# A fused two-layer block on one core: batch 1's value tiles projected one head later and in other PSUM banks

## The chip, the cores and the metric

The kernel runs on one core of one Trainium2 chip. The metric is device microseconds for one execution of the whole kernel. A trace of one execution was taken by the hardware profiler; the engines are TensorE (PE, with its weight loads PEld), VectorE (DVE), ScalarE (ACT), GpSimd (POOL) and SyncE (SP, which issues the DMA transfers).

## The reference, cut to what matters

The block runs cross-attention, a quantised feed-forward, a second attention layer that has a self-attention ("a1") and a cross-attention ("a2"), each with its own feed-forward, and a last feed-forward. The change lies wholly within the self-attention a1: 2 batches, 512 tokens of 128 features, 16 heads of 32 features, so 32 pairs of batch and head.

```python
xn = _ln(x, lnx_g, lnx_b)
yn = _ln(y, lny_g, lny_b)
q = jnp.einsum('bsc,hcd->bhsd', xn, wq)
k = jnp.einsum('btc,hcd->bhtd', yn, wk)
v = jnp.einsum('btc,hcd->bhtd', yn, wv)
a = jax.nn.softmax(jnp.einsum('bhsd,bhtd->bhst', q, k) * D ** (-0.5), axis=-1)
if causal:
    a = a * mask
o = jnp.einsum('bhst,bhtd->bhsd', a, v)
```

For a1, x and y are the same tensor and `causal` is true; the mask keeps only keys after the query (`t > s`).

## The kernel before, in words

The order of the work is written out by hand, one program per engine; an engine runs its instructions in that order and waits on semaphores. There are eight PSUM banks of 128 x 512 values: S0 to S3 for the scores, T0 and T1 for transposes, A and B for the rest. A bank is claimed by TensorE (`claim`), which waits until the bank's last reader has released it.

In a1 the loop runs over n = 0 to 33; head n (below, "head 8" is n = 8) is a pair of batch and head, 16 heads of batch 0 first. Per head:

- TensorE multiplies four tiles of queries with all keys (`scores`, L702, banks S0 to S3, one per tile). The float32r operands lie in `stack`, where each head's high and low halves of q and k are stacked.
- VectorE takes each row's negated maximum (L1647); ScalarE computes the exponential with its row sum (L1247); GpSimd masks the diagonal block (L1009).
- One head later TensorE transposes the ten kept 128 x 128 blocks of the weights (`p_transposes`, L444 with `pring`) in three sets of 4, 3 and 3 blocks. The sets alternate between T0 and T1 (`next_T`). ScalarE copies the first set into the ring PT (L1231), VectorE the second (L1619), and the third goes to ScalarE after an odd head, to VectorE after an even one.
- Every four heads form a group k. At n % 4 == 1 TensorE transposes the inverse row sums (`sums_transposes`, L444 with `xn`, bank A), ScalarE copies them (`sums_across`, L1211); at n % 4 == 2 and 3 the weighted values follow in bank A (`values`, L738), and VectorE multiplies the two (`normalise`, L1639).

Beside this loop the operands of later heads are made. At even n from 6 to 20 one 128 x 512 projection of q or k is computed in bank B (`project`, L688); in the next head ScalarE writes its high half (L1203), VectorE its low half (`low_half`, L1592), and when a set of four projections is complete, SyncE stacks the halves with four transfers per pair of heads (L884, 256 KB each). Head 8, 16 and 24 are the first ones to read the next stacked set, and each waits for it by a semaphore (`stacked[0]`).

The values V of 8 tiles of 128 tokens are projected by `project_values` (one float32 projection, 128 x 512, in two passes, L761). Tiles 0 to 3 (batch 0) come ahead of the loop and in head 0. Tiles 4 to 7 (batch 1) are given by `value_tile(n)`: in the kernel before at n = 8, 12, 16 and 20, in bank A, which is free then between the weighted values of one group and the sums of the next. They are copied in the head that follows, n = 9, 13, 17 and 21: even tiles by ScalarE (L1216) behind its copy of the first set of transposes, odd ones by VectorE (L1599) behind its copy of the second set. The first reader of tiles 4 to 7 is the weighted values of head 22.

```python
def next_T():
    turn[0] += 1
    return f"T{turn[0] % 2}"

def project_values(t, res):
    pe.wait_ge(ynT_ready, t // NT + 1)
    claim(pe, res, ("v", t), read_by=((V_act, V_dve)[t % 2], t // 2 + 1))
    filled(pe.matmul(bank(res), ynT[:, t // NT, t % NT * P:(t % NT + 1) * P], wa1_sb[:, 2, :],
                     start=True, stop=True), ("v", t))
```

Of the kernel before, what the change touches and what calls it, by code (L numbers as in the profile page):

```python
# [39 lines left out]
NT = 4  # L40
# [42 lines left out]
def build(nc, x, ctx_in, w64, w128, wf0, wa1, wa2, wa2kv, wf1, rows, cols, out):  # L83
    with ExitStack() as st:
# [104 lines left out]
        def bank(res):  # L189
            return ps[:, BANKS[res], :]  # L190
# [60 lines left out]
        def claim(pe, res, key, read_by=None, filled_by=None):  # L251

            if res in last:
                pe.wait_ge(*last[res])
            if read_by is None:
                frees[res] += 1
                read_by = (bank_free[res], frees[res])
            if filled_by is None:
                fulls[res] += 1
                filled_by = (bank_full[res], fulls[res])  # L260
            where[key], filled_when[key], read_when[key], last[res] = res, filled_by, read_by, read_by

        def filled(ins, key):

            return ins.then_inc(filled_when[key][0], 1)
# [149 lines left out]

        def value_tile(n):

            return NT + n // 4 - 2 if n % 4 == 0 and 8 <= n <= 20 else None

        def pt_base(n):  # L420

# [18 lines left out]
        def _(pe):  # L440
# [249 lines left out]
            def scores(n, i):  # L690

                b, j, e, _ = head(n)
                claim(pe, f"S{i}", ("s1", n, i), read_by=(exp1_done, NT * n + i + 1))
                if i == 0:
                    if n < 2:

                        pe.wait_ge(first_stack[n], 16 * 4)
                    elif e == 0:

                        t = n // (2 * HG)  # L700
                        pe.wait_ge(stacked[j], stack_count(t, j))
                filled(pe.matmul(bank(f"S{i}"), stack[:, j, 0, e, i * P:(i + 1) * P], stack[:, j, 1, e, :],  # L702
                                 start=True, stop=True), ("s1", n, i))
# [47 lines left out]
            def sums_transposes(k):  # L751
                pe.wait_ge(rdx_ready, k + 1)
                res = "A" if k < NGRP - 1 else "B"
                claim(pe, res, ("rt", k), read_by=(RT_ready, k + 1))
                transposes(("rt", k), res, lambda t: rdx[:, t, :, :].rearrange("p h d -> p (h d)"), NT)
# [7 lines that stand above are left out]
# [19 lines left out]
            for n in range(NHB + 2):  # L782
                k = n // HG - 1
                if n < NHB:
                    scores(n, 0)
                    scores(n, 1)
                if 1 <= n <= NHB:
                    p_transposes(n - 1, 0)
                    p_transposes(n - 1, 1)
                if n >= HG and n < NHB and n % HG == 3:  # L790
                    values(k, (2,))
                if n == 0:
                    project_values(2, "T0")
                if n < NHB:
                    scores(n, 2)
                    scores(n, 3)
                if n == 0:
                    project_values(3, "T1")
                if 1 <= n <= NHB:
                    p_transposes(n - 1, 2)  # L800
                if n >= HG and n % HG == 1:
                    sums_transposes(k)
                if n >= HG and n % HG == 2:
                    values(k, (3,))
                if n >= HG and n < NHB and n % HG == 3:
                    values(k, (1, 0))
                if n == NHB + 1:
                    values(k, (3, 2, 1, 0))
                for m, res in next_projections(n):
                    project(m, res)  # L810
                if n == 4:
                    ln_transposes("a1", 1)
                if value_tile(n):
                    project_values(value_tile(n), "A")
                if n == NHB:
                    li1(0)

# [217 lines left out]
        def _(act):  # L1035
# [177 lines left out]
            def copy_values(t):  # L1213
                key = ("v", t)
                res = await_bank(act, key)
                release(act.activation(V[:, t, :], bank(res), ACT.Copy), key)  # L1216
# [21 lines left out]
            for n in range(NHB + 2):  # L1238
                if 1 <= n <= NHB:
                    pt_copy(n - 1, 0)  # L1240
                if value_tile(n - 1) and value_tile(n - 1) % 2 == 0:
                    copy_values(value_tile(n - 1))
                for u in range(2):
                    if n < NHB:
                        for i in range(2 * u, 2 * u + 2):
                            act.wait_ge(nm1_ready, NT * n + i + 1)
                            release(act.activation(pring[:, n % 2, i, :], bank(f"S{i}"), ACT.Exp,  # L1247
                                                   bias=nm1[:, n % 8, i:i + 1], accum_out=den1[:, n % 8, i:i + 1]),
                                    ("s1", n, i))
                    if u == 0 and 1 <= n <= NHB and n % 2 == 0:  # L1250
                        pt_copy(n - 1, 2)
                    if u == 0:
                        for m, _ in next_projections(n - 1):
                            high_half(m)
                    if u == 0 and n in (5, 6):
                        a1_evac(1, "qk"[n - 5])
                if n == 0:
                    copy_values(2)
                if n >= HG and n % HG == 1:
                    sums_across(n // HG - 1)  # L1260

# [25 lines left out]
        def _(dve):  # L1287
# [297 lines left out]
            def low_half(m):  # L1585

                which, e, t = projection(m)
                scale = float(D1) ** -0.5 if which == "q" else 1.0
                dve.wait_ge(hi_ready, m + 1)
                halves_free(dve, m)  # L1590
                res = await_bank(dve, ("qk", m))
                ins = dve.scalar_tensor_tensor(part(which + "l", t)[:, e, :], bank(res), scale,  # L1592
                                               part(which + "h", t)[:, e, :].bitcast(F32), ALU.mult, ALU.subtract)
                release(ins, ("qk", m))

            def copy_values(t):
                key = ("v", t)
                res = await_bank(dve, key)
                release(dve.tensor_copy(V[:, t, :], bank(res)), key)  # L1599
# [42 lines left out]
            for n in range(NHB + 2):  # L1642
                for u in range(2):
                    if n < NHB:
                        for i in range(2 * u, 2 * u + 2):
                            await_bank(dve, ("s1", n, i))
                            dve.tensor_reduce(nm1[:, n % 8, i:i + 1], bank(f"S{i}"), AX.X, ALU.max,  # L1647
                                              negate=True).then_inc(nm1_ready, 1)
                    if 1 <= n <= NHB and (u == 0 or n % 2):
                        pt_copy(n - 1, 1 + u)  # L1650
                    if u == 0 and HG <= n <= NHB and n % HG == 0:
                        inverse_sums(n // HG - 1)
                    if u == 0 and value_tile(n - 1) and value_tile(n - 1) % 2:
                        copy_values(value_tile(n - 1))
                for m, _ in next_projections(n - 1):
                    low_half(m)
                if n == 0:
                    copy_values(3)
                    ln_stats("a1", 1, x1)
                if n == 2:  # L1660
                    ln_norm("a1", 1, x1)
                if n >= HG and n < NHB and n % HG == 3:
                    normalise(n // HG - 1)
                if n == NHB:

                    for j in range(HG):
                        dve.wait_ge(stacked[j], stack_count(3, j))
                    for b in range(NB):
                        did(dve.tensor_tensor(xb[:, b, :, :], x1[:, b, :, :], row4("a1_li1_b"), ALU.add))
                    settle()  # L1670

                    add_to_xb(0, "li1")
                    ln_stats("a1f", 0, xo)
                if n == NHB + 1:
                    normalise(NGRP - 1)
# [127 lines left out]
```

## Time and profile before

| what | us |
|---|---|
| median of 3 runs | 386.19 (384.49 to 387.12) |
| profiled execution, whole time | 386.85 |
| its span, first to last instruction | 385.1 |
| TensorE busy in the span | 330.1 (86%) |
| VectorE busy | 285.7 (74%) |
| ScalarE busy | 271.5 (70%) |
| GpSimd busy | 122.7 (32%) |

The trace's times are counted from the span's start. Busy times are shares of the whole span, an average over stages with different limits. Matmuls are pipelined: the duration of one includes the time until its result has left the array, so several in a row overlap, and the start of the next tells more than the end of the last. A row's idle time is that of its engine ahead of it, with the instruction that ended it. In the trace head 8 starts at 152.58 us, head 12 at 169.48, head 16 at 185.87, head 20 at 202.77 and head 24 at 219.26; the value copies are those at 158.29 and 191.6 (ScalarE) and at 175.60 and 208.90 (VectorE).

### The profile page before, as it was taken

To read this page: it belongs to the slowest core of one execution; us is meant where nothing else is said; L and a number is where in the kernel's file an instruction comes from. 1 tells how busy PE (TensorE), PEld (TensorE's weight loads), DVE (VectorE), ACT (ScalarE), POOL (GpSimd) and SP (SyncE) were. 2 spreads that over 40 slices of the span, in tenths; PEclk is the share of its full clock that TensorE was granted. 3 is DMA by queue.
4 is the path that set the end of the run, shared out by engine and by line. 5 is a ranking of instruction groups with operands and counts; after the bars stand their busy time and mean duration, and the time that the engine had idled before them with its cause. 6 is when DMAs were issued, how large, how long until landed. Compare 5 with 4: busy or idle time off the path is not lost.

```text
span 385.1 us, 6932 instructions
## 1 busy us (share of the span) xinstructions
PE 330.1 (86%) x2165; PEld 233.5 (61%) x2165; DVE 285.7 (74%) x736; ACT 271.5 (70%) x957; POOL 122.7 (32%) x227
## 2 busy tenths in 40 slices
PE   5989999717698888898999889899896999978993
PEld 4868887503334554555646555576674888765673
DVE  0767779597886995979979889855586887846515
ACT  2378897847364998989999899914248888754441
POOL 1317665236512332223233233311023533421200
PEclk9999999968898999999999999999998999999999
DMA  6900000000019869403970896000000000000001
GB/s 197 361 9 1 2 3 0 0 1 3 0 43 211 184 143 211 84 2 69 212 159 1 178 212 214 3 2 0 2 2 1 1 2 0 3 0 2 0 2 54
DMA packets 6908, 24.75 MB, mean 64 GB/s; under 512 B 1451, under 2 KB 1528, under 8 KB 6136
## 3 DMA queue, kind: packets, MB, share of 16 engines
q1 hardware_dynamic: 6872, 24.31, 26.3%
q8 instruction: 18, 0.29, 0.3%
q14 instruction: 18, 0.15, 0.1%
HBM read 7.00 MB, written 0.52 MB: 20 GB/s over the span
## 4 chain that ended last, share of the span: by engine, by line
PE 45%; DVE 23%; ACT 16%; DMA 5%; issue 5%; SPq 3%; POOL 1%; DVEq 0%; ACTq 0%
PE ps L444 7%; PE ps L568 7%; PE ps L546 7%; ACT pring L1247 6%; PE ps L626 5%; PE ps L608 5%; DVE nm L1647 4%; PE ps L475 3%; SPq L884 3%; ACT arena L1121 3%; PE ps L496 3%; DMA stack<-sides 3%; PE ps L702 2%; ACT arena L1231 2%; PE ps L738 2%
## 5 line engine op out<-in xcount | busy, mean ns | idle before, releaser
L1647 DVE TENSOR_REDUCE nm<-ps 128x1 f32<-128x512 f32 x128 | 81.2, 678 | 17.0 <-PE ps L702 17.0
L1247 ACT ACTIVATE pring<-ps,nm 128x512 f32<-128x512 f32 x128 | 89.0, 725 | 6.4 <-DVE nm L1647 6.4
L1121 ACT ACTIVATE arena<-ps,nmx 128x77 f32<-128x77 f32 x256 | 79.2, 344 | 14.4 <-DVE nmx L1417 14.1
L1009 POOL TENSOR_SCALAR_AFFINE_SELECT pring<-pring 128x128 f32<-128x128 f32 x128 | 37.4, 295 | 80.9 <-ACT pring L1247 80.9
L702 PE MATMUL ps<-stack 128*128 128x512 f32 x128 | 55.2, 491 | 5.8 <-ACT pring L1247 2.4
L1121 ACT ACTIVATION_READ_ACCUMULATOR arena<-ps,nmx 128x1 f32 x256 | 57.2, 223 | 0.0
L974 POOL TENSOR_TENSOR arena<-arena,rden 128x616 f32<-128x616 f32 x32 | 39.2, 1226 | 51.3 <-DVE rden L1426 51.3
L444 PE MATMUL ps<-ident,pring 128*128 128x128 f32 x320 | 46.9, 275 | 5.9 <-ACT arena L1231 4.3
L444 PEld LDWEIGHTS ps<-ident,pring 128*128 128x128 f32 x320 | 36.5, 140 | 19.8 <-POOL pring L1009 10.7
L568 PEld LDWEIGHTS ps<-arena 128*128 128x128 f32 x320 | 38.9, 191 | 13.1 <-DVE arena L1433 11.7
L568 PE MATMUL ps<-arena 128*128 128x128 f32 x320 | 42.5, 280 | 4.9 <-DVE arena L1433 4.9
L965 POOL TENSOR_TENSOR rstd<-var,minus_half 128x4 f32<-128x4 f32 x18 | 18.8, 1045 | 86.5 <-DVE var L1319 86.5
L546 PE MATMUL ps<-arena,xnT 128*128 128x308 f32 x128 | 39.7, 434 | 2.8 <-ACT arena L1121 1.8
L702 PEld LDWEIGHTS ps<-stack 128*128 128x128 f32 x128 | 22.2, 190 | 27.6 <-ACT pring L1247 16.5
L1433 DVE COPY arena<-ps 128x384 f32<-128x384 f32 x64 | 28.0, 478 | 11.9 <-PE ps L444 11.9
L1231 ACT ACTIVATE arena<-ps 128x512 f32<-128x512 f32 (+1 forms) x48 | 28.6, 595 | 8.7 <-PE ps L444 8.7
L1417 DVE TENSOR_REDUCE nmx<-ps 128x8 f32<-128x616 f32 x32 | 25.5, 797 | 8.6 <-PE ps L546 8.2
L1247 ACT ACTIVATION_READ_ACCUMULATOR pring<-ps,nm 128x1 f32 x128 | 31.1, 243 | 0.0
L1147 ACT ACTIVATE hid<-ps,cols_sb 128x512 f32<-128x512 f32 x24 | 16.3, 686 | 20.1 <-PE ps L608 20.1
L444 PE MATMUL ps<-ident,arena 128*128 128x128 f32 x200 | 28.2, 277 | 1.6 <-POOL arena L974 0.6
L546 PEld LDWEIGHTS ps<-arena,xnT 128*128 128x128 f32 x128 | 22.2, 193 | 9.6 <-ACT arena L1121 2.8
L1619 DVE COPY arena<-ps 128x384 f32<-128x384 f32 x48 | 26.2, 546 | 0.1
(149 smaller groups left out, 525.9 us busy)
## 6 DMA issues: line engine op xcount, KB each, us to landing
stack<-sides SPq DMA_DIRECT2D x32, 256.0 KB, 5.0
stack<-arena SPq DMA_DIRECT2D x16, 256.0 KB, 5.1
stack<-hid SPq DMA_DIRECT2D x12, 256.0 KB, 5.0
wa_sb<-in_wa SPq DMA_DIRECT2D x1, 1536.0 KB, 14.1
early<-in_w SPq DMA_DIRECT2D x2, 512.0 KB, 8.0
stack<-hid SPq DMA_DIRECT2D x8, 128.0 KB, 2.5
arena<-in_wa SPq DMA_DIRECT2D x1, 1024.0 KB, 4.8
pring<-in_wf SPq DMA_DIRECT2D x1, 768.0 KB, 10.7
```

The source lines that it names most:

```text
L444: m = pe.transpose(bank(res)[0:width, t * parts:(t + 1) * parts], src(t), ident[0:parts, 0:parts])
L546: m = pe.matmul(bank(res)[:, 0:4 * HS].rearrange("p (h s) -> p h s", s=HS)[:, :, 0:M], xnT[:, b, t * P:(t + 1) * P], FK[:, b, c0:c0 + 4 * ...
L568: m = pe.matmul(bank(res)[:, t * P:(t + 1) * P], PTc[:, j % 4, k, :], VO[:, b, half * (NCH // 2) + k, :], start=(half == 0 and k == 0), st ...
L702: filled(pe.matmul(bank(f"S{i}"), stack[:, j, 0, e, i * P:(i + 1) * P], stack[:, j, 1, e, :], start=True, stop=True), ("s1", n, i))
L974: pool.tensor_tensor(pv, pv, rden[:, j % 4, :].unsqueeze(2).to_broadcast([P, 8, M]), ALU.mult).then_inc(pn_ready, 1)
L1009: pool.affine_select(out=blk, in_=blk, compare_op=ALU.is_gt, fill=0.0, base=0, pattern=[[1, P]], channel_multiplier=-1).then_inc(masked, 1)
L1121: ins = act.activation(Pc[:, i % PC_SLOTS, h * HS:h * HS + M], bank(where[key])[:, h % 4 * HS:h % 4 * HS + M], ACT.Exp, bias=nmx[:, i % 4, ...
L1231: release(act.activation(pt_piece(n, piece), src, ACT.Copy), key)
L1247: release(act.activation(pring[:, n % 2, i, :], bank(f"S{i}"), ACT.Exp, bias=nm1[:, n % 8, i:i + 1], accum_out=den1[:, n % 8, i:i + 1]), ( ...
L1433: release(dve.tensor_copy(PTc[:, j % 4, k0:k1, :].rearrange("p k n -> p (k n)"), bank(res)[:, 0:(k1 - k0) * P]), key)
L1619: release(dve.tensor_copy(pt_piece(n, piece), src), key)
L1647: dve.tensor_reduce(nm1[:, n % 8, i:i + 1], bank(f"S{i}"), AX.X, ALU.max, negate=True).then_inc(nm1_ready, 1)
```

## The change

`value_tile` now names n = 9, 13, 17 and 21. The projection takes the next bank of the weights' transposes instead of bank A. The copies move to the same n: on ScalarE behind the head's last exponential and ahead of the copy of the sums, on VectorE behind the low halves of the projection.

```diff
         def value_tile(n):
 
-            return NT + n // 4 - 2 if n % 4 == 0 and 8 <= n <= 20 else None
+            return NT + n // 4 - 2 if n % 4 == 1 and 9 <= n <= 21 else None
...
                 if value_tile(n):
-                    project_values(value_tile(n), "A")
+                    project_values(value_tile(n), next_T())
...
                 if 1 <= n <= NHB:
                     pt_copy(n - 1, 0)
-                if value_tile(n - 1) and value_tile(n - 1) % 2 == 0:
-                    copy_values(value_tile(n - 1))
                 for u in range(2):
...
                 if n == 0:
                     copy_values(2)
+                if value_tile(n) and value_tile(n) % 2 == 0:
+                    copy_values(value_tile(n))
                 if n >= HG and n % HG == 1:
                     sums_across(n // HG - 1)
...
                         inverse_sums(n // HG - 1)
-                    if u == 0 and value_tile(n - 1) and value_tile(n - 1) % 2:
-                        copy_values(value_tile(n - 1))
                 for m, _ in next_projections(n - 1):
                     low_half(m)
+                if value_tile(n) and value_tile(n) % 2:
+                    copy_values(value_tile(n))
```

On TensorE, the rows from the end of head 8 to the transposes of the sums in head 9 stood as follows. L688 is the projection of q or k, L761 that of the value tile 4, L702 the scores, L444 with `pring` the transposes of the weights and with `xn` those of the sums; in brackets are the semaphores that a row waits for (`V_act` and `V_dve` are counted up by the value copies, `pt_act` and `pt_dve` by the copies of the transposed weights, `exp1_done` by the exponentials).

```order
L688 MATMUL ps<-ynT,wa1_sb 128x512 [waits lo_ready,ynT_ready]
L761 MATMUL ps<-wa1_sb,ynT 128x512 [waits OT_ready,ynT_ready]
L702 MATMUL ps<-stack 128x512 [waits exp1_done] x2
L444 MATMUL ps<-ident,pring 128x128 [waits pt_dve,masked]
L444 MATMUL ps<-ident,pring 128x128 x3
L444 MATMUL ps<-ident,pring 128x128 [waits pt_act,masked]
L444 MATMUL ps<-ident,pring 128x128 x2
L702 MATMUL ps<-stack 128x512 [waits exp1_done] x2
L444 MATMUL ps<-ident,pring 128x128 [waits pt_act,masked]
L444 MATMUL ps<-ident,pring 128x128 x2
L444 MATMUL ps<-ident,xn 128x128 [waits V_act,rdx_ready]
L444 MATMUL ps<-ident,xn 128x128 x3
```

Here are the changed kernel's rows of the same engine from the third set of head 8's transposes to the second set of head 9's.

```order
L444 MATMUL ps<-ident,pring 128x128 [waits pt_act,masked]
L444 MATMUL ps<-ident,pring 128x128 x2
L444 MATMUL ps<-ident,xn 128x128 [waits OT_ready,rdx_ready]
L444 MATMUL ps<-ident,xn 128x128 x3
L761 MATMUL ps<-wa1_sb,ynT 128x512 [waits pt_dve,ynT_ready]
L702 MATMUL ps<-stack 128x512 [waits stacked1,exp1_done]
L702 MATMUL ps<-stack 128x512 [waits exp1_done]
L444 MATMUL ps<-ident,pring 128x128 [waits pt_dve,masked]
L444 MATMUL ps<-ident,pring 128x128 x3
L444 MATMUL ps<-ident,pring 128x128 [waits V_act,masked]
L444 MATMUL ps<-ident,pring 128x128 x2
```

The projection has moved from ahead of head 9's scores to behind the sums' transposes; the wait for the value copy has moved from those to the second set of head 9's transposes.

On VectorE, this is the difference in heads 13 and 14 (tile 5): L1647 are the maxima, L1619 the copies of the weights' transposes, L1592 the low half, L1599 the value copy.

```order
 L1647 TENSOR_REDUCE nm<-ps 128x1 x4
 L1619 COPY arena<-ps 128x3x128
+L1647 TENSOR_REDUCE nm<-ps 128x1 x2
+L1619 COPY arena<-ps 128x3x128
+L1592 SCALAR_TENSOR_TENSOR arena<-ps,arena 128x512
 L1599 COPY early<-ps 128x512
 L1647 TENSOR_REDUCE nm<-ps 128x1 x2
 L1619 COPY arena<-ps 128x3x128
-L1592 SCALAR_TENSOR_TENSOR arena<-ps,arena 128x512
-L1647 TENSOR_REDUCE nm<-ps 128x1 x2
-L1619 COPY arena<-ps 128x3x128
```

The value copy now stands behind two maxima, a copy and the low half, and ahead of the maxima of head 14. Heads 21 and 22 read the same, with `sides` in place of `arena` in the low half's row.

## Rows read from the trace of the kernel before

**Rows 1.** Busy time by stretch: us, then each engine's, clock, DMA share, GB/s

```profile
86.00:88.00 2.00, 1.44 (x7) 0.86 (x8) 0.51 (x2) 1.19 (x2) 1.40 (x1) 0.50 0.00 0
...
152.50:169.50 17.00, 16.02 (x115) 9.62 (x107) 14.71 (x27) 15.85 (x45) 5.23 (x17) 1.00 0.31 67
...
202.80:219.30 16.50, 14.41 (x109) 9.16 (x105) 15.94 (x29) 15.48 (x43) 5.72 (x19) 1.00 0.37 77
```

**Rows 2.** Chain of waits, two pieces: start us, us, what

```profile
162.54 0.50 ACT arena L1231
...
213.98 5.15 DMA stack<-sides
```

**Rows 3.** Timeline of TensorE, heads 8 to 13: start, us, instruction, idle before, releaser

```profile
154.88 1.02 PE L688 MATMUL ps<-ynT,wa_sb 128*128 128x512 f32 x2
155.74 1.02 PE L761 MATMUL ps<-wa_sb,ynT 128*128 128x512 f32 x2
...
159.04 0.63 PE L444 MATMUL ps<-ident,xn 128*128 128x128 f32 x4
...
160.28 0.50 PE L702 MATMUL ps<-stack 128*128 128x512 f32 x1 [0.17 <-ACT pring L1247]
160.62 0.93 PE L444 MATMUL ps<-ident,pring 128*128 128x128 f32 x7
...
162.11 0.51 PE L702 MATMUL ps<-stack 128*128 128x512 f32 x1 [0.17 <-ACT pring L1247]
163.18 0.52 PE L444 MATMUL ps<-ident,pring 128*128 128x128 f32 x3 [0.56 <-ACT arena L1231]
...
176.43 0.63 PE L444 MATMUL ps<-ident,xn 128*128 128x128 f32 x4 [0.47 <-DVE early L1599]
...
177.36 1.25 PE L444 MATMUL ps<-ident,pring 128*128 128x128 f32 x7
...
179.59 0.52 PE L444 MATMUL ps<-ident,pring 128*128 128x128 f32 x3 [0.52 <-ACT arena L1231]
```

**Rows 4.** Timeline of ScalarE, heads 9 and 13

```profile
158.29 0.61 ACT L1216 ACTIVATE early<-ps 128x512 f32<-128x512 f32 x1
...
161.89 0.65 ACT L1211 ACTIVATE xn<-ps 128x512 f32<-128x512 f32 x1
162.37 0.66 ACT L1231 ACTIVATE arena<-ps 128x512 f32<-128x512 f32 x1
...
176.51 0.62 ACT L1203 ACTIVATE arena<-ps 128x512 fp32r<-128x512 f32 x1
...
178.79 0.65 ACT L1231 ACTIVATE arena<-ps 128x512 f32<-128x512 f32 x1
```

**Rows 5.** Timeline of TensorE, first scores of head 24

```profile
219.26 0.70 PE L702 MATMUL ps<-stack 128*128 128x512 f32 x2 [0.88 <-DMA stack<-sides]
```

**Rows 6.** Timeline of VectorE, heads 10 and 13

```profile
165.81 1.29 DVE L1647 TENSOR_REDUCE nm<-ps 128x1 f32<-128x512 f32 x2 [1.51 <-PE ps L702]
...
175.60 0.68 DVE L1599 COPY early<-ps 128x512 f32<-128x512 f32 x1
176.20 1.28 DVE L1647 TENSOR_REDUCE nm<-ps 128x1 f32<-128x512 f32 x2
...
177.86 0.68 DVE L1592 SCALAR_TENSOR_TENSOR arena<-ps,arena 128x512 fp32r<-128x512 f32 x1
```

**Rows 7.** Timeline of VectorE, the low half in head 21

```profile
211.15 0.68 DVE L1592 SCALAR_TENSOR_TENSOR sides<-ps,sides 128x512 fp32r<-128x512 f32 x1
```

**Rows 8.** Timeline of SyncE's issues, 205 to 222 us

```profile
211.91 11.11 SPq L884 DMA_DIRECT2D stack<-sides  x10
```

**Rows 9.** Timeline of TensorE in the quantised feed-forward

```profile
85.27 0.61 PE L527 MATMUL ps<-identb,pring 128*128 128x128 bf16 x4 [4.96 <-ACT pring L1103]
86.56 1.03 PE L519 MATMUL ps<-wf0b,pring 128*128 128x512 bf16 x2 [0.69 <-ACT pring L1108]
...
91.13 0.59 PE L519 MATMUL ps<-wf0b,pring 128*128 128x512 bf16 x2
```

## Prediction

> **What bounds the kernel now.** I read the page's first part, then the busy time by stretch, the chain of waits, and last the timelines of the engines. On the page TensorE is the busiest engine, with VectorE and ScalarE not far behind; but shares of the whole span say little here, because all of the change lies between head 8 and head 24 of the first self-attention. So I cut that stretch at the first scores of every fourth head and read the busy time [rows 1]: of the 17.00 us of heads 8 to 11 TensorE works 16.02, ScalarE 15.85 and VectorE 14.71; heads 20 to 23 have TensorE at 14.41 of 16.50. All three are close to the bound, so moving work between queues without removing any can only win what somebody waits for. TensorE's granted clock is 1.00 in both, its upper level of 2.4 GHz.
>
> Who waits for whom is in the chain of waits [rows 2]. In the group of heads 8 to 11 it runs through ScalarE until its copy of head 9's first weights (L1231, 162.37), and goes over to TensorE at 163.18, which waited for that copy [rows 2, 3]. None of ScalarE's rows from 158.29 to that copy names idle time ahead of it [rows 4]. Before head 24 the chain lies on a transfer: the stacked halves of batch 1's second pair of groups land at 219.13, and TensorE, idle for 0.88 us, starts head 24 at 219.26 [rows 2, 5].
>
> **What the change touches there, and the sum.** Nothing is added or removed: four projections, four copies. The pairs of heads are 8 to 10 and 16 to 18 (tiles 4, 6, copied by ScalarE), 12 to 14 and 20 to 22 (tiles 5, 7, copied by VectorE); I work out one of each, the other repeats it in the trace to 0.1 us.
>
> The projection. A key projection of the same shape starts at 154.88 and the value projection behind it at 155.74, so one takes 0.86 us of TensorE's stream [rows 3]. It leaves the end of head 8. That is worth nothing there: ScalarE is full and VectorE's rows run on, so earlier scores of head 9 only lie in their banks longer. It comes back behind the transposes of the sums (159.04). There TensorE waits three times before 163.18: 0.17, 0.17 and 0.56, together 0.90 [rows 3]. So 0.86 fits.
>
> ScalarE, tile 4. Its copy holds a slot of 0.48 us at 158.29. It moves behind the last exponential of head 9, and what stood between slides 0.48 earlier; so it runs from 161.89 - 0.48 = 161.41 to 162.02 (it lasts 0.61). The sums' copy still starts at 161.89 and the copy of head 9's first weights at 162.37, because the work ahead of both is the same [rows 4]. The cost on ScalarE is 0.
>
> The new wait. The tile now occupies a bank of the weights' transposes, and the next but one in that ring, head 9's second set, must wait for the copy. Behind it in TensorE's queue stand head 10's last two scores, head 9's third set and the weighted values. A copy by ScalarE that started at 162.37 and lasted 0.66 let TensorE go at 163.18, so a release costs 0.15 us [rows 3, 4]. The second set then starts at 162.02 + 0.15 = 162.17. Seven transposes last 0.93 and three 0.52, so one takes 0.10 of the stream and three 0.31; one score lasts 0.50 and two 0.70, so two take some 0.42 [rows 3, 5]. TensorE is at the third set at 162.90. That set cannot start before 163.18 in either kernel, since it waits for the copy of 162.37. So the wait is covered with 0.28 to spare. VectorE copies the second set later by what TensorE brings it later, and sits idle for 1.51 us some rows on, which takes that up [rows 6]. Sum for tiles 4 and 6: 0, bounded below by 0 (ScalarE is full) and above by the whole new wait: TensorE would be at the second set at 161.14 (159.04 and 0.41 for the sums, 0.86, 0.42, and 0.41 for the first set), 1.03 before it may start. I take 0, because the row of 163.18 covers it.
>
> VectorE, tile 5. The copy leaves its slot of 0.60 (175.60 to 176.20), so what follows slides 0.60 earlier; the low half at 177.86 could start at 177.26, but needs ScalarE's high half, 176.51 + 0.62 + 0.15 = 177.28. So it gains 0.58, and the copy itself runs at 177.86 to 178.54; the maxima of head 14 follow at 178.46 as before (177.86 and a slot of 0.60) [rows 4, 6]. On TensorE the transposes of the sums no longer wait 0.47 for the copy (176.43), but the projection's 0.86 now stands behind them: 175.96 + 0.41 + 0.86 + 0.42 puts the first set of head 13 at 177.65 instead of 177.36. It is through at 178.06; the second set waits for the copy until 178.54 + 0.15 = 178.69; with 0.31 and 0.42 TensorE is at the third set at 179.42, and that starts at 179.59 anyway, behind the copy of 178.79 [rows 3, 4]. Sum 0, with only 0.17 to spare; bounds: -0.47 (the wait goes and nothing takes its place) and +0.63 (178.69 less 178.06).
>
> The low half at head 21. Here the same 0.58 counts. The low half at 211.15 is the last thing for which the transfer to head 24's stack waits: SyncE issues at 211.91, four transfers, landed at 219.13 [rows 2, 7, 8]. TensorE waited 0.88 for them, so a landing 0.58 earlier starts head 24 0.58 earlier, and up to 0.30 of delay from heads 20 to 23 would be swallowed by the same wait. ScalarE and VectorE have nothing to do then but wait for TensorE. Head 16's transfer also starts 0.58 earlier, but TensorE does not wait for it: 0. Bounds: 0 and -0.58; I take -0.58, since the wait stands in the row.
>
> Sum: 0 + 0 - 0.58 = -0.58 us. The profiled execution took 386.85 us, 1.75 outside its span of 385.1; it would be 386.27. The median of the runs is 386.19, 0.66 below the profiled one, and goes to 385.6.
>
> A rule that speaks against the change: the Trainium skill, "TensorE: Matmul & The Clock Gate", section "A second HAM failure mode: psum-queue depth-cycling", says that a kernel which cycles PSUM banks can pause TensorE often and briefly enough that its clock falls and rises again. By that rule the ring of two banks with one more tenant could cost clock; the groups with waits of 0.17 to 0.88 us show a granted clock of 1.00 [rows 1, 3, 5], so the trace does not bear it out here, and the sum by it would be the third rival's.
>
> **Rivals.**
> 1. The copy holds the bank longer than worked out: the wait takes the place of those removed. Place: the second transposes of heads 9, 13, 17. It decides as soon as a copy ends more than 0.28 (ScalarE) or 0.17 (VectorE) later than above. For it: the margins are smaller than one copy; VectorE's copy is now last in its head. Against: ScalarE's work ahead is unchanged. Unabsorbed, 1.03 + 0.63 + 1.03 = 2.7 (head 22's falls into the wait of head 24): 386.19 + 2.7 = 388.9, slower; half absorbed, 387.5.
> 2. The removed waits count in full: 2 x 0.47 + 0.58 = 1.5, so 384.7. For it: they stand in the rows. Against: TensorE must do 0.86 of projection in the same place.
> 3. TensorE's clock falls to its lower level (1.2 GHz) behind the new pauses. In the quantised feed-forward ahead of the attention it did, where TensorE had been without work for 4.96 us (0.50 granted in the stretch that follows): two matmuls of 512 columns then lasted 1.03 us, and 0.59 once the clock was back [rows 1, 9], 1.75 times less. Some 3.6 us of TensorE's work in a head would grow by 0.75 x 3.6 = 2.7, less the 0.9 of waits 1.8; in the four heads behind the four tiles 7.2: 393.4. Against: no pause worked out above is longer than 1.03.
> 4. The earlier transfer brings nothing (its four issues or the memory set the landing) and the rest is 0: 386.2.
>
> **How the numbers follow.** Forecast 0.56, rival 1 0.17, rival 2 0.10, rival 3 0.02, rival 4 0.15. The forecast is 385.6. The three runs lie 1.7 below and 0.9 above the median, so a median of new runs may be off by some 0.7: rival 2 less that is 384.0, rival 1 is inside up to 388.4, all but its unabsorbed end; only that, rival 3 and the tails of new runs are left out. One per cent is 3.9 us, about what a measurement of this kernel can tell from no change. Only rival 3, and rival 1 unabsorbed in a bad set of runs, go beyond on the slow side (0.03); on the fast side nothing in the rows is worth 3.9, and 0.02 is left for what I have not seen.
>
> **What would show it.** The transposes of the sums of heads 13 and 21 should have no wait on VectorE's value copy; the second transposes of heads 9, 13, 17 and 21 should show a wait for a value copy (L1216's and L1599's place), and the third ones still a wait for ScalarE's copy, shorter or gone on TensorE but starting no later. The groups of four heads should keep their lengths to within 0.2, and the one before head 24 should lose about 0.6, with VectorE's low half ahead of the copy. The prediction is wrong if a group of heads 8 to 19 changes by more than 0.5 us, if head 24's wait stays at 0.88 with an unchanged landing, or if the granted clock leaves 1.00.

## The result and the profile after

| kernel | median us | runs | profiled execution | span |
|---|---|---|---|---|
| before | 387.63 (384.49 to 388.84) | 20 | 386.85 | 385.1 |
| changed | 384.56 (383.93 to 388.49) | 20 | 383.94 | 382.2 |

The ratio given for the comparison is 0.9950 with a 95% interval of 0.9929 to 0.9971: less than one per cent faster. It is not the quotient of the two medians, which is 0.992. The runs gather in groups some 2 us apart, so a median can jump from one group to the next: the means (387.37 and 385.36) lie 2.0 us apart, the medians 3.07. The forecast was 385.6 in a range of 384.0 to 388.4. The median of before, 386.19 over 3 runs, became 387.63 over 20, so the difference that the forecast named (0.58 us) and the difference of the medians (3.07) have to be compared apart from the absolute time.

So the first reading is where the two profiled executions differ, cut at the first scores of every fourth head. This is the busy time by stretch of the changed kernel (columns as in [rows 1]; the stretches run from head 0 to 8, then to 12, 16, 20 and 24).

```profile
115.84:150.19 34.35, 29.44 (x164) 17.53 (x164) 29.84 (x62) 30.74 (x82) 10.33 (x32) 1.00 0.92 194
150.19:167.09 16.90, 15.65 (x111) 9.37 (x107) 14.54 (x27) 15.73 (x45) 5.19 (x17) 1.00 0.31 68
167.09:183.47 16.38, 15.64 (x110) 9.35 (x106) 15.02 (x28) 15.24 (x43) 5.19 (x17) 1.00 0.41 84
183.47:200.35 16.88, 15.63 (x110) 9.36 (x106) 14.53 (x27) 15.73 (x45) 5.19 (x17) 1.00 0.81 169
200.35:216.11 15.76, 14.87 (x109) 9.01 (x105) 15.26 (x29) 14.99 (x43) 5.29 (x18) 1.00 0.38 80
```

The kernel before, cut at its own heads (152.58, 169.48, 185.87, 202.77, 219.26), has 16.90, 16.39, 16.90 and 16.49. Three groups keep their length to 0.02; the fourth loses 0.73. From head 8 to head 24 that is 66.68 against 65.92, or 0.76. The remaining 2.1 us of the two spans' difference of 2.9 lie where no instruction was changed: 2.39 ahead of head 8, and 0.28 given back behind head 28. Of the 2.39, 1.53 lie between head 0 and head 8 (35.88 against 34.35). First the kernel before, the whole stretch and two microseconds of it, then the same two microseconds of the changed kernel.

```profile
116.70:152.58 35.88, 31.87 (x165) 18.31 (x165) 29.95 (x62) 30.71 (x82) 10.35 (x32) 0.95 0.88 186
118.00:120.00 2.00, 2.00 (x4) 1.01 (x3) 1.40 (x3) 1.56 (x5) 0.59 (x2) 0.50 1.00 215
```

```profile
118.00:120.00 2.00, 2.00 (x7) 0.91 (x5) 2.00 (x6) 2.00 (x7) 0.88 (x4) 1.00 1.03 205
```

The granted clock stood at 0.50 (1.2 GHz) in one execution and at 1.00 (2.4 GHz) in the other, with the same instructions. Whether the change has a part in that is the question of the repeated runs below. Nine of the twelve traces of this case come from kernels with the same instructions up to head 0. From 118 to 120 us the clock was 1.00 in three of them (the changed kernel twice and the later copies) and 0.50 or 0.62 in six, of which four have some or all of the projections moved as well.

What the change did is read from heads 9, 13 and 21. TensorE, heads 9 and 13 and the start of head 24:

```profile
156.52 0.60 PE L444 MATMUL ps<-ident,xn 128*128 128x128 f32 x4
156.95 1.02 PE L761 MATMUL ps<-wa_sb,ynT 128*128 128x512 f32 x2
...
159.81 0.52 PE L444 MATMUL ps<-ident,pring 128*128 128x128 f32 x3 [0.94 <-ACT early L1216]
...
160.78 0.52 PE L444 MATMUL ps<-ident,pring 128*128 128x128 f32 x3
...
173.41 0.60 PE L444 MATMUL ps<-ident,xn 128*128 128x128 f32 x4
...
176.20 0.52 PE L444 MATMUL ps<-ident,pring 128*128 128x128 f32 x3 [0.44 <-DVE early L1599]
...
177.19 0.52 PE L444 MATMUL ps<-ident,pring 128*128 128x128 f32 x3
...
216.11 0.70 PE L702 MATMUL ps<-stack 128*128 128x512 f32 x2
```

The transposes of the sums (L444 with `xn`) no longer wait for VectorE's value copy, where [rows 3] had 0.47. The second sets carry the new wait for a value copy: 0.94 behind ScalarE's, 0.44 behind VectorE's. The third sets (160.78, 177.19) have no idle time named in their rows (the smallest that any row of this text names is 0.16), but with the 2.39 us by which head 8 starts earlier they stand at 163.17 and 179.58 of the old count, where [rows 3] had 163.18 and 179.59. So the new wait lies wholly beside the old one. Head 24 starts without an idle time in its row, where [rows 5] had 0.88. VectorE in head 21 shows why:

```profile
203.58 2.42 DVE L1647 TENSOR_REDUCE nm<-ps 128x1 f32<-128x512 f32 x4
...
207.57 0.55 DVE L1619 COPY arena<-ps 128x384 f32<-128x384 f32 x1
208.04 0.69 DVE L1592 SCALAR_TENSOR_TENSOR sides<-ps,sides 128x512 fp32r<-128x512 f32 x1
208.65 0.68 DVE L1599 COPY early<-ps 128x512 f32<-128x512 f32 x1
```

The low half now stands ahead of the value copy, 7.69 us behind head 20's start (200.35) where [rows 7] had it 8.38 behind (211.15 less 202.77): 0.69 earlier. The chain of waits follows it through SyncE's issue into head 24:

```profile
208.13 0.62 DVE sides L1592
...
208.81 0.58 SPq L884
...
210.88 5.09 DMA stack<-sides
215.97 0.14 issue
216.11 0.70 PE ps L702 x2
```

The transfer still ends the chain into head 24, at 215.97, and lasts about as long as before (5.15 in [rows 2]). It only starts earlier.

### The profile page after: what moved, and what is told of

It reads as the page before. It is cut to its first block, busy times and chain, and to the rows that moved or that the text cites. A ratio compares the mean times of both kernels' runs of the same rounds, so it can differ in the third digit from the quotient of the medians.

```text
span 382.2 us, 6928 instructions
## 1 busy us (share of the span) xinstructions
PE 327.6 (86%) x2161; PEld 232.2 (61%) x2165; DVE 285.5 (75%) x736; ACT 271.4 (71%) x957; POOL 122.4 (32%) x227
## 4 chain that ended last, share of the span: by engine, by line
PE 44%; DVE 25%; ACT 17%; issue 5%; DMA 4%; SPq 3%; POOL 1%; DVEq 0%; another core or an unknown queue 0%; ACTq 0%
PE ps L444 7%; PE ps L546 7%; PE ps L568 6%; ACT pring L1245 6%; DVE nm L1647 5%; PE ps L626 5%; PE ps L608 5%; PE ps L475 3%; ACT arena L1121 3%; SPq L884 3%; DMA stack<-sides 3%; PE ps L738 3%; PE ps L702 2%; PE ps L496 2%; DVE xn L1326 2%
## 5 line engine op out<-in xcount | busy, mean ns | idle before, releaser
L1647 DVE TENSOR_REDUCE nm<-ps 128x1 f32<-128x512 f32 x128 | 81.1, 681 | 15.5 <-PE ps L702 15.4
L702 PE MATMUL ps<-stack 128*128 128x512 f32 x128 | 54.8, 489 | 5.6 <-DMA stack<-hid 3.4
L444 PE MATMUL ps<-ident,pring 128*128 128x128 f32 x320 | 47.4, 276 | 6.8 <-ACT arena L1231 2.2
L444 PEld LDWEIGHTS ps<-ident,pring 128*128 128x128 f32 x320 | 36.1, 140 | 22.3 <-POOL pring L1009 12.7
L702 PEld LDWEIGHTS ps<-stack 128*128 128x128 f32 x128 | 21.8, 188 | 28.7 <-ACT pring L1245 18.3
L444 PE MATMUL ps<-ident,arena 128*128 128x128 f32 x200 | 28.2, 277 | 1.9 <-POOL arena L974 0.8
L1619 DVE COPY arena<-ps 128x384 f32<-128x384 f32 x48 | 26.4, 550 | 1.3 <-PE ps L444 1.2
```

The lines of the kernel that those rows point to most:

```text
L444: m = pe.transpose(bank(res)[0:width, t * parts:(t + 1) * parts], src(t), ident[0:parts, 0:parts])
L1619: release(dve.tensor_copy(pt_piece(n, piece), src), key)
```

## The experiments

The theory: the whole effect is the place of one low half (head 21's) ahead of one copy; the rest moves without being seen. The rivals: the sum of the removed waits counts; the tiles 4 to 6 gain or lose something; and, for the larger difference of the medians, the change makes the clock fall less often.

**The same kernels again.** Two runs without an edit: the kernel before against itself, and the changed kernel once more.

> The kernel before against itself. Theory A (the change is worth only what its own stretch loses, 0.73 us of 66.7 between the first scores of head 8 and of head 24; the rest of the 2.9 us between the two traces lies ahead of head 8, where both programs are the same, and comes from TensorE's clock and the first loads of that execution): ratio 1.000 with an interval that holds 1, single runs spread over some 4 us as before. Theory B (the spread of the runs is small and the whole ratio of 0.995 is the change's): ratio 1.000 with single runs within about 1 us of each other.

> The changed kernel once more. Theory A: head 8 to head 24 takes 65.9 us, ratio near 0.998 (0.73 of 387), and the stretch ahead of head 8 differs from run to run by up to 2.4 us with the clock. Theory B: ratio again 0.995 or below, also where the stretch ahead of head 8 is the same in the two traces.

Measured: the kernel before against itself 0.9977 (0.9947 to 1.0006; 386.56 over 12 runs), the changed one 0.9973 (0.9939 to 1.0007; 385.59 over 12). The stretches from head 8 to head 24 were 66.62 and 65.90. So the 0.7 us between the heads comes back in the traces to 0.1, and the 3 us of the medians does not (1.2 us in this comparison): the changed kernel's interval can't be told from that of the kernel before against itself. The 0.7 us alone would be a ratio of 0.998, which lies outside the first interval and inside the second; nothing beyond it is confirmed.

**Tile 7 alone, and all but tile 7.** A list of the tiles that are moved; the others stay in head 8, 12, 16 or 20 and in bank A. For all but tile 7 the list is `(4, 5, 6)`. The lines not shown give the listed tiles the places and banks of the changed kernel.

```diff
+        LATE_TILES = (7,)
...
-            return NT + n // 4 - 2 if n % 4 == 0 and 8 <= n <= 20 else None
+            t = NT + n // 4 - 2 if n % 4 == 0 and 8 <= n <= 20 else None
+            return None if t in LATE_TILES else t
...
```

> Only tile 7 (head 20/21) is projected late, in the transposes' banks, and copied behind the low half; tiles 4, 5 and 6 as before. Theory A (the gain is the earlier low half at head 21, so an earlier transfer to head 24's stack): the whole 0.73 is there: heads 8 to 20 take 50.2 us as before, head 20 to 24 takes 15.76, ratio near 0.998. Theory C (the gain needs the waits on the value copies removed at all four places): at most a quarter of it, 0.2 us.

> Tiles 4, 5 and 6 late, tile 7 as before. Theory A: nothing gained: groups of 16.90, 16.38, 16.88 and 16.49 us, TensorE idle for 0.88 us ahead of head 24, ratio 1.000. Theory C: three quarters of the gain, 0.5 us.

Measured, heads 8, 12, 16 and 20 to the next group: tile 7 alone 16.87, 16.40, 16.88, 15.82; all but tile 7 16.88, 16.39, 16.88, 16.43. The medians were 386.6 (0.9977, 0.9942 to 1.0012) and 386.56 (0.9985, 0.9958 to 1.0012), which can't tell them apart; the stretches do. The first scores of head 24, first with tile 7 alone, then with all but tile 7:

```profile
218.79 0.70 PE L709 MATMUL ps<-stack 128*128 128x512 f32 x2 [0.22 <-DMA stack<-sides]
```

```profile
220.63 0.70 PE L709 MATMUL ps<-stack 128*128 128x512 f32 x2 [0.82 <-DMA stack<-sides]
```

Tile 7 alone brings 0.67 of the 0.73 (16.49 less 15.82), and the other three bring nothing that can be told from the scatter of this group, which is 16.43 to 16.49 in the three traces that leave all four tiles in place.

**The copy ahead of the low half.** All of the change, but with VectorE's value copy ahead of the low halves again.

```diff
+                if value_tile(n) and value_tile(n) % 2:
+                    copy_values(value_tile(n))
                 for m, _ in next_projections(n - 1):
                     low_half(m)
-                if value_tile(n) and value_tile(n) % 2:
-                    copy_values(value_tile(n))
```

> The changed kernel, but on VectorE the copies of tiles 5 and 7 stand ahead of the low halves in heads 13 and 21 instead of behind them; projection and banks as in the change. Theory A (the gain of tile 7 is the low half's place alone): the low half of head 21 comes 0.6 us later again, so does the transfer, and heads 20 to 24 take 16.4 us instead of 15.76 with TensorE idle for some 0.6 us ahead of head 24; heads 8 to 20 unchanged. Theory D (the gain of tile 7 is the wait of the sums' transposes that is gone): 15.8 us.

Measured: 16.90, 16.40, 16.90, 16.52, the lengths of the kernel before. There is one run (388.59 us), so only the stretches are read. VectorE in head 21, then the start of head 24:

```profile
210.50 0.69 DVE L1599 COPY early<-ps 128x512 f32<-128x512 f32 x1
211.11 0.68 DVE L1592 SCALAR_TENSOR_TENSOR sides<-ps,sides 128x512 fp32r<-128x512 f32 x1
```

```profile
219.20 0.70 PE L702 MATMUL ps<-stack 128*128 128x512 f32 x2 [0.91 <-DMA stack<-sides]
```

Head 20 starts at 202.68 here, so the low half is back at 8.43 behind it and the wait at 0.91. The later projection and the other bank alone are worth nothing; the order of two instructions on VectorE is the gain.

**Later copies.** To see the price of the longer-held bank, ScalarE's copy was put behind the sums' copy (one slot of 0.48 later) and VectorE's behind the first two maxima of the next head (1.20 later).

```diff
+                if n >= HG and n % HG == 1:
+                    sums_across(n // HG - 1)
                 if value_tile(n) and value_tile(n) % 2 == 0:
                     copy_values(value_tile(n))
-                if n >= HG and n % HG == 1:
-                    sums_across(n // HG - 1)
...
+                    if u == 0 and value_tile(n - 1) and value_tile(n - 1) % 2:
+                        copy_values(value_tile(n - 1))
                     if 1 <= n <= NHB and (u == 0 or n % 2):
                         pt_copy(n - 1, 1 + u)
...
-                if value_tile(n) and value_tile(n) % 2:
-                    copy_values(value_tile(n))
```

> The changed kernel with every value copy later: on ScalarE behind the copy of the sums (0.48 us later), on VectorE behind the first two maxima of the next head (1.20 us later). By the margins of the prediction (0.28 and 0.17 us) the groups of heads 8 and 16 grow by 0.48 - 0.28 = 0.20 us to 17.1, the group of head 12 by 1.20 - 0.17 = 1.03 to 17.4; the group of head 20 grows by less than 1.03, at most to 16.8, since some of it lies in front of the transfer's landing. The rival (the new wait has no cover at all): 0.48, 1.20 and 0.48. Another (the ring of two banks is never the bound): all groups unchanged.

Measured: 17.18, 17.39, 17.19, 16.54, which is 0.28, 1.01, 0.31 and 0.78 more than in the changed kernel (again one run, 385.15 us). TensorE's second sets of heads 9 and 13, and what follows up to the third sets:

```profile
160.13 0.52 PE L444 MATMUL ps<-ident,pring 128*128 128x128 f32 x3 [1.43 <-ACT early L1216]
160.40 0.71 PE L702 MATMUL ps<-stack 128*128 128x512 f32 x2
160.95 0.49 PE L444 MATMUL ps<-ident,pring 128*128 128x128 f32 x3
...
177.52 0.52 PE L444 MATMUL ps<-ident,pring 128*128 128x128 f32 x3 [1.63 <-DVE early L1599]
...
178.33 0.49 PE L444 MATMUL ps<-ident,pring 128*128 128x128 f32 x3
```

What a delay costs less than itself is the margin: 0.48 less 0.28 or 0.31 is 0.17 to 0.20 at ScalarE's tiles, and 1.20 less 1.01 is 0.19 at VectorE's. Rival 1 is a real mechanism, and beyond some 0.2 us it counts in full. At head 21, 0.23 of the delay fits ahead of the transfer's landing.

**All four copies on VectorE.** ScalarE is the full engine in heads 8 to 11 [rows 1, 4], so its copies of tiles 4 and 6 were given to VectorE, behind the low halves as well. The lines not shown ahead of these set the counts that the weighted values wait for.

```diff
...
-                claim(pe, res, ("v", t), read_by=((V_act, V_dve)[t % 2], t // 2 + 1))
+                claim(pe, res, ("v", t), read_by=(V_dve, t - 1) if t >= NT else
+                      ((V_act, V_dve)[t % 2], t // 2 + 1))
...
-                if value_tile(n) and value_tile(n) % 2 == 0:
-                    copy_values(value_tile(n))
...
-                if value_tile(n) and value_tile(n) % 2:
+                if value_tile(n):
                     copy_values(value_tile(n))
```

> The changed kernel with tiles 4 and 6 copied by VectorE too, behind its low halves. If ScalarE's full queue up to the copy of head 9's first weights is what sets the groups of heads 8 and 16, each loses the copy's slot of 0.48 us or a little less (0.3 to 0.48; VectorE's maxima of head 10 come 0.6 us later and may keep a part): 16.4 to 16.6 instead of 16.88. If VectorE or TensorE bounds them as much, they stay at 16.88. Groups of heads 12 and 20 unchanged (16.38, 15.76). Whole time: 0.6 to 1.0 below the changed kernel's.

Measured: 385.05 (383.89 to 385.44, 10 runs), ratio 0.9946 (0.9915 to 0.9978); groups 16.39, 16.39, 16.39, 15.81. It was not run beside the changed kernel, so only the groups are read against it. TensorE in head 9, then ScalarE's copy of head 9's first weights, and last that copy in the changed kernel:

```profile
162.58 0.52 PE L444 MATMUL ps<-ident,pring 128*128 128x128 f32 x3 [0.43 <-DVE early L1598]
...
163.57 0.52 PE L444 MATMUL ps<-ident,pring 128*128 128x128 f32 x3
```

```profile
162.77 0.65 ACT L1232 ACTIVATE arena<-ps 128x512 f32<-128x512 f32 x1
```

```profile
159.98 0.66 ACT L1231 ACTIVATE arena<-ps 128x512 f32<-128x512 f32 x1
```

Head 8 starts at 153.46 here, so the third set stands 10.11 behind it; in the changed kernel it was 10.59 (160.78 less 150.19). ScalarE's copy, for which the third set waits, moved by the same 0.48 (9.31 behind head 8, 9.79 in the changed kernel). The groups of ScalarE's tiles lose some 0.5 each, one slot of its copy. So those groups were bound by ScalarE's queue up to that copy, which the chain in [rows 2] said.

**TensorE kept at work ahead of head 0.** `keep_busy` multiplies without a use for the result while head 0's stacked operands are on their way; 18 such matmuls in place of 10, in the changed kernel and in the kernel before.

```diff
-            keep_busy(10)
+            keep_busy(18)
```

> The changed kernel with 18 instead of 10 matmuls that only keep TensorE busy ahead of head 0 (their result is not used), so that it does not idle for some 2 us on the first stacked transfer. If the 34.35, 35.9 and 37.5 us that head 0 to head 8 took in the traces so far come from the clock that falls behind that pause, this stretch takes 34.3 to 34.5 us in the profile and the runs lie closer together, with a median 0.5 to 1.5 us below the changed kernel's. If the spread has another cause, single runs spread over 4 us as before and the stretch still comes in three lengths.

> The kernel before with the 18 matmuls ahead of head 0 and nothing else. If the pause ahead of head 0 lets the clock fall whatever the value tiles do, head 0 to head 8 takes 34.4 to 34.9 us here too, the groups stay at 16.90, 16.39, 16.90 and 16.5, and the runs centre some 0.7 us above those of the changed kernel with the same matmuls (384.29 in the last comparison): 385.0. If the changed kernel owed its lower spread to the tiles, this one spreads over 384 to 389 as the kernel before.

Measured: in the changed kernel 384.29 (383.29 to 387.07, 12 runs), ratio 0.9935 (0.9906 to 0.9965); in the kernel before 386.58 (385.3 to 388.76, 12 runs), 0.9982 (0.9957 to 1.0008), where 385.0 was expected. The first scores of head 0, in the kernel before and then, with 18 matmuls, in the changed kernel, where head 2 follows below:

```profile
116.70 0.70 PE L702 MATMUL ps<-stack 128*128 128x512 f32 x2 [1.90 <-DMA stack<-hid]
```

```profile
116.35 0.70 PE L702 MATMUL ps<-stack 128*128 128x512 f32 x2 [0.16 <-DMA stack<-hid]
...
125.92 0.70 PE L702 MATMUL ps<-stack 128*128 128x512 f32 x2 [2.79 <-DMA stack<-hid]
```

In both kernels the pause ahead of head 0 is gone and the clock of the stretch from 118 to 120 us is 1.00. But the kernel before still had runs as far apart as without the edit, and those of the changed kernel still lay 3.8 us apart. Its profiled execution shows the next such place: from head 28 to the end it took 153.0 where the first one took 151.3, with a granted clock of 0.82 and 0.75 at the start of a2's cross-attention. The same place in the kernel with the copy first, the same matmuls at the lower clock (0.50 granted from 297.52 to 299.58) and, some 5 us on, at the upper one (1.00 from 302.57 to 303.61):

```profile
297.52 2.26 PE L546 MATMUL ps<-arena,xnT 128*128 128x308 f32 x4
...
302.57 1.21 PE L546 MATMUL ps<-arena,xnT 128*128 128x308 f32 x4
```

So the pause ahead of head 0 was taken away, a second place was found, and the theory that head 0's pause alone sets the spread fell.

**Both.** All four copies on VectorE and 18 matmuls ahead of head 0.

> The changed kernel with all four tiles copied by VectorE and the 18 matmuls. The two act in different stretches, so they add: head 0 to head 8 34.4 to 34.9, groups of 16.39, 16.39, 16.39 and 15.81, and a median 0.9 to 1.0 below that of the 18 matmuls alone: 383.3. If the two are not independent, a group or the stretch ahead shows it.

Measured: 383.37 (381.74 to 386.41, 9 runs), ratio 0.9912 (0.9879 to 0.9945); groups 16.40, 16.39, 16.40, 15.73. It has the lowest median of all, with an interval below 1 throughout; it was not run against the changed kernel on the same chip, so that it beats it by 1.2 us is a comparison of two medians. Its profiled execution met the clock elsewhere. The start of head 2, and the granted clock behind it:

```profile
126.29 0.70 PE L702 MATMUL ps<-stack 128*128 128x512 f32 x2 [2.73 <-DMA stack<-hid]
```

```profile
128.00:130.00 2.00, 2.00 (x7) 1.22 (x6) 2.00 (x6) 2.00 (x7) 0.58 (x2) 0.50 1.00 205
```

Heads 0 to 8 took 37.95 here, against 34.90 in the kernel with 18 matmuls alone, which had paused 2.79 at that place and kept 1.00.

## Why the prediction was right, and where its sizes were off

**The groups ahead of head 20: right.** Sum 0 was forecast for tiles 4, 5 and 6, and the groups moved by 0.02 at most; all but tile 7 alone shows the same. With the shift of 2.39 the working can be laid on the rows: the second set of head 9 was forecast at 162.17 and came at 162.20 (159.81), with a wait of 0.94 where 1.03 was worked out; that of head 13 at 178.69 and came at 178.59 (176.20), with 0.44 where it was 0.63. The third sets came as in the kernel before.

**The margins: one mis-sized.** 0.28 was worked out for ScalarE's tiles and 0.17 for VectorE's; the later copies measured 0.17 to 0.20 and 0.19. The term that was mis-sized is the "0.42" for two scores, which was taken from the durations of rows. By the start of the next row, where the third set follows without a wait, the later copies have 0.82 of work between the second set and the third (160.13 to 160.95) and 0.81 in head 13 (177.52 to 178.33), where 0.73 was taken. Three transposes are 0.27 of it (160.13 to 160.40), and the two scores 0.55 (160.40 to 160.95). In the changed kernel the two sets lie 0.97 and 0.99 apart (159.81 to 160.78, 176.20 to 177.19). For VectorE's tile this is made good by the second set, which came 0.10 earlier than forecast. A slip of 0.02 in the working changes nothing: the copy was set 0.58 behind the low half (177.28 to 177.86), whose slot is 0.60.

**The low half: right in place, 0.15 too small.** Forecast 0.58, measured 0.69 at the low half and 0.73 over the group. Two terms were off. The release from ScalarE to VectorE was taken as 0.15, read from a wait of TensorE on ScalarE [rows 3, 4]; here ScalarE's high half ended at 208.01 and VectorE's low half started at 208.04, so the release took 0.03 at most. And "That is worth nothing there", said of the projection leaving the end of head 20, was not wholly so: the four maxima of head 21 took 2.42 us where the kernel before had 2.51, since the scores came earlier. ScalarE's high half in the changed kernel:

```profile
207.39 0.62 ACT L1203 ACTIVATE sides<-ps 128x512 fp32r<-128x512 f32 x1
```

**The rivals.** Rival 1 (the bank held longer) did not occur where the copies are put, and the later copies show that it would have a price. Rival 2 (the removed waits count in full) fell, though the 384.7 that it gave is nearer to the measured median than the forecast's 385.6: the 0.47 of head 13 and the 0.17 to 0.56 of head 9 went away and the groups kept their length. Rival 3 (the clock) did not occur in heads 8 to 23, where every group has 1.00 behind pauses of 0.44 and 0.94 us. Beside this, the Trainium skill, "TensorE: Matmul & The Clock Gate", section "A second HAM failure mode: psum-queue depth-cycling", speaks of a clock that falls where banks are cycled with many short pauses; no group with the added tenant shows it here. Rival 4 (the earlier transfer brings nothing) fell with tile 7 alone and with the copy first.

**What was left out.** That 384.56 lies in the forecast's range is in part luck. The forecast of 0.58 is a ratio of 0.9985, which lies outside the measured interval; the mechanism that was forecast is shown for 0.73 us between the heads, and what lies beyond it was neither forecast nor explained. The forecast took the spread of three runs as the spread of the median. Twenty runs moved before's median up by 1.44, twice the 0.7 that was allowed. The cause lies outside the change: three places where the same instructions take different times in different executions. Head 0 to head 8 took 34.35, 35.9 or 37.5 us in the traces with 10 matmuls ahead of it; head 28 to the end 150.5 to 153.1; the start of head 0 came between 115.66 and 116.92. Single runs of the kernel before gather near 384.4, 386.5 and 388.5 in the first three comparisons; how these three places add up to that was not worked out. Whether the change shifts how often the clock falls stays open: of 20 runs each, 11 of the changed kernel and 1 of the kernel before lay at or below 384.6 in the first comparison, but 4 of 12 and 7 of 35 in the second. Counted at a bound that a gain of 0.7 does not carry a group across, above 387.3, it is 1 of 20 against 10 of 20, and 3 of 12 against 15 of 35. That leans towards fewer long executions of the changed kernel, but nothing here shows by what the change would bring them about.

## What to carry to other kernels

Where an engine feeds a transfer that somebody waits for, put the instruction that completes the operands ahead of work that only frees a buffer: that order alone was worth 0.7 us here, while four moved projections and a changed bank were worth nothing. A wait that is removed counts only if nothing else ends at the same point; look for the next wait in that engine's queue and subtract. And where a gain is below the spread of single runs, cut both traces at the same events and compare the stretches: they came back to 0.1 us where the medians moved by 1 to 3.

## What the runs showed of the hardware that was not expected

In these traces the granted clock is not set by the length of TensorE's pause alone. Behind 1.90 us without work ahead of head 0 it went to 0.50 in the kernel before, and behind 1.98 us at the same place it stayed at 1.00 in the changed kernel; with all copies on VectorE a pause of 1.88 was followed by 0.53 (116 to 118 us), with the later copies one of 1.89 by 1.00; ahead of head 2 a pause of 2.73 us was followed by 0.50 and one of 2.79 us by 1.00. Where it fell, heads 0 to 8 took 1.5 to 3.2 us longer, about the size of the whole measured difference.

A release through a semaphore is not of one size: 0.15 us from ScalarE's copy to TensorE [rows 3, 4], and at most 0.03 us from ScalarE's high half to VectorE's low half in the rows above.
